# Linear attention layers and the input pass: normed rows and K turned in blocks of 32 by VectorE and moved by SBUF transfers, in place of TensorE transposes

## The reference

```
# block 0: 16 heads of 32; block 1: 8 heads of 64 (linear attention)
xn = layernorm(x)
q = softmax(xn @ Wq + bq, over a head's features)
k = softmax(xn @ Wk + bk with masked rows at -inf (block 1: -1e6), over the 512 rows)
v = (xn @ Wv + bv) * keep
attn = k^T v for each head;  y = q @ attn
x = x + silu(layernorm(y) * (1 + scale) + shift) @ Wo + bo
# block 2: the same frame with ordinary softmax attention, 16 heads
# block 3: xn = layernorm(layernorm(x) * ada_scale + ada_shift); products of xn (mx, delta,
# B, C rows); two selective state-space scans over the rows; gated output projection
```

## Time and profile before

| | |
|---|---|
| median of 3 runs | 5685.93 us (5684.82 to 5686.73) |
| the profiled execution | 5681.6 us |
| its span in the profile | 5679.5 us |
| mean granted TensorE clock | 0.989 of full |
| TensorE matmul busy | 5410.8 us (95%) |
| VectorE busy | 4209.2 us (74%) |
| ScalarE busy | 2919.1 us (51%) |
| GpSimd busy | 2906.6 us (51%) |

### The profile page before, as it was taken

How to read it: one execution, slowest core, us unless ns; L and a number is a source line. 1 busy time by engine, 2 the same in 40 slices (tenths; PEclk the granted TensorE clock), 3 DMA queues, 4 the chain that set the end, 5 groups by cost and what they waited for, 6 DMA issues and landing times. The chain is left out here.

```text
span 5679.5 us, 136465 instructions
## 1 busy us (share of the span) xinstructions
PE 5410.8 (95%) x58478; PEld 3262.1 (57%) x58478; DVE 4209.2 (74%) x5904; ACT 2919.1 (51%) x4944; POOL 2906.6 (51%) x956
## 2 busy tenths in 40 slices
PE   8999989998999999978989999999999999999998
PEld 3555545554455555544445566666666666666665
DVE  1456545554466666673349999999999999999996
ACT  0122212222455555551247776777777677677774
POOL 0000000000000000003449999999999999999997
PEclk9999999999999999998999999999999999999999
DMA  6200021001000000004431111112111121201211
GB/s 237 80 34 33 32 71 34 31 29 65 11 1 20 17 21 17 21 20 164 167 120 50 52 34 62 65 60 69 54 43 55 60 67 54 73 24 62 65 59 33
DMA packets 146330, 321.90 MB, mean 57 GB/s; under 512 B 27721, under 2 KB 28362, under 8 KB 135514
## 3 DMA queue, kind: packets, MB, share of 16 engines
q1 hardware_dynamic: 142866, 308.25, 16.1%
q10 hardware_dynamic: 2896, 5.34, 0.3%
HBM read 238.66 MB, written 74.89 MB: 55 GB/s over the span
## 5 line engine op out<-in xcount | busy, mean ns | idle before, releaser
L2070 POOL TENSOR_TENSOR sc_state<-sc_state,sc_c_rows 128x2048 f32<-128x2048 f32 x512 | 2330.2, 4564 | 122.8 <-DVE sc_state L2381 121.4
L2381 DVE TENSOR_TENSOR_SCAN sc_state<-sc_decay,wide 128x512 f32<-128x512 f32 x2048 | 2335.2, 1198 | 28.0 <-PE wide L2240 20.8
L2240 PEld LDWEIGHTS wide<-sc_diag,sc_du_t 64*64 64x64 f32 x32768 | 1048.0, 133 | 527.0 <-issue 344.0
L2240 PE MATMUL wide<-sc_diag,sc_du_t 64*64 64x128 f32 x32768 | 1218.9, 272 | 19.9 <-DVE sc_state L2381 19.7
L2256 PE MATMUL wide<-sc_state,half 64*64 64x512 f32 x8192 | 1199.5, 592 | 7.5 <-POOL sc_state L2070 7.0
L2174 ACT ACTIVATE sc_decay<-sc_delta,neg_a 128x512 f32<-128x512 f32 x1024 | 723.6, 719 | 448.7 <-DVE sc_state L2381 443.6
L2174 ACT ACTIVATE sc_decay<-sc_delta_x,neg_a 128x512 f32<-128x512 f32 x1024 | 710.1, 717 | 286.7 <-DVE sc_state L2381 282.5
L2256 PEld LDWEIGHTS wide<-sc_state,half 64*64 64x64 f32 x8192 | 405.8, 133 | 168.6 <-issue 127.5
L1491 DVE CUSTOM_DVE_ANT_0 l_prob<-wide,l_mask_add 128x512 f32<-128x512 f32 x512 | 339.6, 682 | 211.6 <-PE wide L1323 211.4
L1232 ACT ACTIVATE l_prob<-l_prob,l_s_max 128x512 f32<-128x512 f32 x512 | 366.0, 716 | 250.4 <-DVE l_s_max L1491 250.4
L2213 PE MATMUL wide<-set 128*128 128x512 f32 x1024 | 476.2, 608 | 0.0
(11 more groups left out here) (244 smaller groups left out, 6912.6 us busy)
## 6 DMA issues: line engine op xcount, KB each, us to landing
sc_c_rows<-c_d SPq DMA_DIRECT2D x64, 1024.0 KB, 4.8
set<-wz_tiles SPq DMA_DIRECT2D x128, 256.0 KB, 2.7
x<-ahead_out SPq DMA_DIRECT2D x24, 1024.0 KB, 4.8
ahead_x_wk<-x SPq DMA_DIRECT2D x16, 1024.0 KB, 5.7
sc_mx<-mx_d SPq DMA_DIRECT2D x64, 256.0 KB, 2.7
mx_d<-fr_mx SPq DMA_DIRECT2D x14, 1024.0 KB, 4.4
pro_wc<-in_wcT SPq DMA_DIRECT2D x4, 2048.0 KB, 19.2
xn_d<-fr_xn_t SPq DMA_DIRECT2D x8, 1024.0 KB, 4.2
```

Source lines behind the costliest of these rows:

```text
L2070: pool.tensor_tensor(state[quad % STATES][:, :, :], state[quad % STATES][:, :, :], c_rows[(r * 4 + q) % ROWS][:, :, :], ALU.mult).then_inc ...
L2240: last = pe.matmul(to[cols_to, k, :, :], du_t[slot % 2][rows, k, of * 64:(of + 1) * 64], diag[r % 2][rows, c, k, :, :], start=True, stop=True)
L2381: dve.tensor_tensor_scan(state[quad % STATES][:, step % 4, order], decay[step % DECAYS][:, order], pair[:, i, order], 0.0, ALU.mult, ALU.a ...
```

## The change

In the two linear layers the stages TK and T leave TensorE. VectorE instead turns blocks of 32x32 within a tile (`turn_x`, `turn_k`; four instructions of 128x512 each), and SyncE moves the blocks to their partitions with 16 SBUF-to-SBUF transfers of 64 KB for x (`move_x`) and 16 for K (`move_k`). Each transfer goes from 32 partitions to 32 partitions with runs of 128 floats (512 bytes). ScalarE then scales the moved rows from SBUF into `xn_t`, undoing the order of the blocks by its access pattern. K's features are dealt out by fours on the host (`by_fours`), so that K's turned blocks come out in runs of 128 floats as well. K is scaled by the reciprocal of its sums in both layers, by four VectorE instructions at the end of the batch before, and the drain of A loses the scale in layer 1. The first `xn` of a layer is still turned by TensorE, in the banks of stage Y. The input pass does the same for the normed rows of batches 1 to 7: VectorE turns them behind the normed rows, SyncE moves them (`move_blocks`), and ScalarE scales them (`scaled`) behind the seventh of the eight SiLU drains of the batch before.

```diff
-        plan = [("V", 4, "dve"), ("TK", 4, "act"), ("TQ", 4, "act"), ("A", 4, "dve"), ("Y", 4, "dve"),
-                ("T", 4, "act"), ("K", 4, "dve"), ("TY", 4, "act"), ("Q", 4, "dve"), ("O", 4, "dve")]
+        plan = [("V", 4, "dve"), ("TQ", 4, "act"), ("A", 4, "dve"), ("Y", 4, "dve"),
+                ("K", 4, "dve"), ("TY", 4, "act"), ("Q", 4, "dve"), ("O", 4, "dve")]
...
+                def move_x(b):
+                    sp.wait_ge(x_turned, (b + 1) * TT)
+                    for i in range(4):
+                        for q in range(4):
+                            sp.dma_start(xn[q * 32:(q + 1) * 32, :, i * P:(i + 1) * P],
+                                         x_blocks[i * 32:(i + 1) * 32, q, :, :, :].rearrange("c k t r -> c k (t r)")
+                                         ).then_inc(x_moved, 16)
+                def move_k(b):
+                    sp.wait_ge(k_turned, (b + 2) * DT)
+                    if not isinstance(b, int) or b >= 0:
+                        sp.wait_ge(psum_full, st.full(b, "A", DT - 1))
...
                         load(b + 2, j)
+                        move_x(b)
+                        move_k(b)
                     sp.wait_ge(out_ready, (b + 1) * TT)
...
                 def next_norms(b):
+                    act.wait_ge(x_moved, (b + 1) * 256)
+                    act.sem_inc(passed, 1)
+                    act.wait_ge(psum_full, st.full(b, "V", TT - 1))
                     for k in range(DT):
-                        drain(b, "T", k, xn_t[:, k, :], ACT.Identity, scale=col(NW, k), bias=col(NB, k))
+                        act.activation(xn_t[:, k, :].rearrange("p (t i r) -> p t i r", t=TT, i=4),
+                                       xn[:, k, :].rearrange("p (i t r) -> p t i r", t=TT, i=4), ACT.Identity,
+                                       scale=col(NW, k), bias=col(NB, k)).then_inc(xn_t_ready, 1)
...
                 def next_k(b):
-                    pe.wait_ge(xn_ready, (b + 2) * TT)
-                    transposes(pe, b, "T", xn)
-                    pe.wait_ge(*wait_drained(b, "T", DT - 1))
                     if isinstance(b, int) and b < 0:
+                        pe.wait_ge(xn_ready, TT)
+                        transposes(pe, b, "Y", xn)
                         pe.wait_ge(w_ready[1], 16)
+                    pe.wait_ge(xn_t_ready, (b + 2) * DT)
                     project_t(pe, b, "K", wk)
...
                     if linear:
-                        pe.wait_ge(k_norm_ready if layer == 0 else k_exp_ready, (b + 1) * DT)
-                        transposes(pe, b, "TK", k_t)
                         pe.wait_ge(q_exp_ready, (b + 1) * TT)
                         transposes(pe, b, "TQ", q_tm)
                         pe.wait_ge(v_ready, (b + 1) * TT)
-                        pe.wait_ge(*wait_drained(b, "TK", TT - 1))
+                        pe.wait_ge(k_moved, (b + 1) * 256)
...
+                def turn_x(b):
+                    for t in range(TT):
+                        dve.wait_ge(xn_ready, b * TT + t + 1)
+                        dve.sem_inc(passed, 1)
+                        dve.transpose(x_blocks[:, :, :, t, :].rearrange("p q k r -> p k q r"), xn[:, t, :]
+                                      ).then_inc(x_turned, 1)
+                def turn_k(b):
+                    dve.wait_ge(k_exp_ready, (b + 2) * DT)
+                    dve.sem_inc(passed, 1)
+                    dve.reciprocal(k_sum[:, :], k_sum[:, :]).then_inc(rk_ready, 1)
+                    dve.wait_ge(rk_ready, b + 2)
+                    for k in range(DT):
+                        dve.tensor_scalar(k_t[:, k, :], k_t[:, k, :], k_sum[:, k:k + 1], None, ALU.mult
+                                          ).then_inc(k_norm_ready, 1)
+                    if not isinstance(b, int) or b >= 0:
+                        dve.wait_ge(k_moved, (b + 1) * 256)
+                    for k in range(DT):
+                        dve.wait_ge(k_norm_ready, (b + 1) * DT + k + 1)
+                        dve.sem_inc(passed, 1)
+                        dve.transpose(k_blocks[:, :, :, :, k].rearrange("p q t r -> p t q r"), k_t[:, k, :]
+                                      ).then_inc(k_turned, 1)
...
                     norms(b + 1, pair + j, 1 - j)
...
+                    if not last:
+                        turn_x(b + 1)
...
                         next_k(b)
                         next_q(b)
+                        turn_k(b)
                     dve.wait_ge(xb_ready, b + 1)
...
+                    if b + 1 < B:
+                        move_blocks(b + 1)
                     parts = 4 if b == B - 1 else 2
...
+                def scaled(b):
+                    act.wait_ge(blocks_moved, b * 256)
...
+                        if m == 6 and b + 1 < B:
+                            scaled(b + 1)
...
+                    for t in range(TT):
+                        dve.wait_ge(xn_ready, b * TT + t + 1)
+                        dve.transpose(turned[:, :, :, t, :].rearrange("p j k r -> p k j r"), xn[j][:, t, :]
+                                      ).then_inc(blocks_turned, 1)
```

More of the change, by code:

```diff
@@ L490, in attention_layer @@
         pt_full, pt_ready, pv_done, y_drained = sem("pt_full"), sem("pt_ready"), sem("pv_done"), sem("y_drained")
+        x_turned, x_moved, k_turned, k_moved = sem("x_turned"), sem("x_moved"), sem("k_turned"), sem("k_moved")
+        xn_t_ready = sem("xn_t_ready")
         def wait_bank(pe, b, name, k):
@@ L680, in _ @@
                     sp.dma_start(scan["half"][:, :], d["half_ident"]).then_inc(scan["const_loaded"], 16)
+                def move_x(b):
[9 more added lines that the diff above has]
+                        sp.wait_ge(psum_full, st.full(b, "A", DT - 1))
+                    for i in range(4):
+                        for q in range(4):
+                            sp.dma_start(k_tm[q * 32:(q + 1) * 32, :, i * P:(i + 1) * P],
+                                         k_blocks[i * 32:(i + 1) * 32, q, :, :, :].rearrange("c t r m -> c t (r m)")
+                                         ).then_inc(k_moved, 16)
                 def body(b, pair, j, more):
@@ L783, in body @@
                     if linear:
-                        for t in range(TT):
-                            drain(b, "TK", t, k_tm[:, t, :], ACT.Copy)
                         for k in range(DT):
@@ L877, in body @@
                     project(pe, b, "O", h_t, wo)
-                first = [i[0] for i in plan].index("T")
+                first = [i[0] for i in plan].index("Y")
                 absent(st, pe, psum_full, "pe", -1, plan[0][0], first)
@@ L895, in _ @@
                 dve.sem_inc(xn_ready, TT)
-                first = [i[0] for i in plan].index("T")
+                first = [i[0] for i in plan].index("K")
                 absent(st, dve, drained["dve"], "dve", -1, plan[0][0], first)
@@ L921, in norms @@
                     dve.wait_ge(rstd_ready, b + 1)
-                    if not isinstance(b, int) or b > 0:
-                        dve.wait_ge(psum_full, st.full(b - 2, "T", DT - 1))
+                    dve.wait_ge(xn_t_ready, b * DT)
                     for t in range(TT):
@@ L958, in body @@
                     norms(b + 1, pair + j, 1 - j)
-                    if linear:
-                        dve.wait_ge(k_exp_ready, (b + 1) * DT)
-                        dve.reciprocal(k_sum[:, :], k_sum[:, :]).then_inc(rk_ready, 1)
-                        dve.wait_ge(rk_ready, b + 1)
-                        if layer == 0:
-                            for k in range(DT):
-                                dve.tensor_scalar(k_t[:, k, :], k_t[:, k, :], k_sum[:, k:k + 1], None, ALU.mult
-                                                  ).then_inc(k_norm_ready, 1)
+                    if not last:
+                        turn_x(b + 1)
                     for t in range(TT):
@@ L1030, in _ @@
                 next_q(-1)
+                turn_k(-1)
                 absent(st, dve, drained["dve"], "dve", -1, "O", 1)
@@ L2476, with by_fours @@
     s = lambda key: v["L3_cond_" + key]
+    def by_fours(layer, a):
+        return a if layer == 2 else a.reshape(a.shape[:-1] + (P, 4)).swapaxes(-1, -2).reshape(a.shape)
     def crossed(a):
```

89 lines of the change are left out of this document (55 added, 34 removed).

## The result

The changed kernel took 5713.16 us (median of 5 runs, 5709.2 to 5715.7), the kernel before 5685.93 us on the same chip: the ratio is 1.0045, with a 95% interval of 1.0031 to 1.0059. It is slower, where I had forecast 5614 us and at most 5660. The profiled execution after took a span of 5707.1 us, 27.6 more than the 5679.5 before.

What follows compares the result with a forecast made beforehand. TensorE, busy 96 to 97% in the changed stages, was taken as the bound. Gains of 48.7 + 17.7 + 5.0 + 0.9 = 72.3 us gave 5614 us; forecast 5590 to 5632, wider range 5588 to 5660.

Steps and rivals of the forecast that it cites:

- T's 3.48 us: Linear layers, end of Y to K: stage T with its drain goes, 3.48 us in each of 14 batches, 48.7 us.
- GpSimd's lock on V's scaling: Linear layers: the V scaling that meets GpSimd's addition takes 4.03 us instead of 0.49, standing still until GpSimd is done.
- The input pass's chain: Input pass: VectorE turns, SyncE moves, ScalarE scales the normed rows; it takes back TensorE's 25 us, leaving 0.9 us gained.
- its floor of 5590: Whole kernel: the time with every wait in the input pass gone, 24 us under the forecast of 5614.
- I take 0.45 per transfer: SyncE's queue: each small transfer issued 0.45 us after the last; the layers' wait stays hidden up to 0.56 us.
- GpSimd's addition waits for the store, but not before the next normed rows: Linear layers: the store queued behind K's 16 transfers on SyncE does not delay GpSimd's addition; costed at nothing.
- the first product should wait for ScalarE about 3 us per batch: Input pass, sign in the new trace: TensorE's first product waits about 3 us and the period stays near 38.3.
- A late by 1.9 or 3.7 us: First batch of each layer: turning K ahead of the norms makes A later by 1.9 in layer 0, 3.7 in layer 1.
- K by 4.3 in the rival: Linear layers, slower-queue rival: at an issue interval of 0.85 us K waits 4.3 us in each of 14 batches, 60 us.
- turning K: VectorE, first batch of a layer: four block transposes at 0.69 us each, within 4.85 us of added work before A.
- the forecast 71 us: Both linear layers: the summed gain, 48.7 from stage T, 17.7 from layer 0's V to A and 5.0 from layer 1's.
- The queue sets the pace: Rival on SyncE's transfers: issues every 0.85 us give 5716 us; queue slower than 0.6 had chance 0.28, of which 0.12 slower.

Runs made afterwards that it cites:

- e2: The changed kernel with the layers' store of each batch's result issued by ScalarE instead of SyncE behind K's 16 transfers: 5693.2 us, ratio 1.0012 to the kernel before.
- e8: The changed kernel with e3, e5 and e4 together, and half of the layers' transfers of x issued by ScalarE: 5604.5 us, ratio 0.986 to the kernel before.
- e5: e2 with VectorE's loop over the batches of the linear layers written out: 5672.6 us, ratio 0.9976 to the kernel before.
- e1: The changed kernel with its input pass put back as before the change, layers still changed: 5679.3 us, ratio 0.9988 to the kernel before.
- e4: The changed kernel with each 64 KB transfer written as one run of 2 KB per partition instead of four of 512 bytes: 5701.4 us, ratio 1.0027.
- e7: The changed kernel with half of the input pass's 16 transfers issued by ScalarE, half by SyncE: 5667.6 us, ratio 0.997 to the kernel before.
- e3: The changed kernel with the input pass's normalising and turning ahead of three drains, and its transfers ahead of three small stores: 5661.7 us, ratio 0.9959.
- e9: The changed kernel with only VectorE's loop of the linear layers written out, store left on SyncE: 5699.4 us, ratio 1.0023 to the kernel before.

## Why the prediction was wrong

**What held.** T's 3.48 us are gone and K follows Y, without a wait behind 11 of 14 batches. A block transpose of `x` takes 0.68 us, also under GpSimd's addition (e2). Landing is 2.0 to 2.1 us. GpSimd's lock on V's scaling is there. The input pass's chain is built as I wrote it. And the gain that I summed up is there to be had: e8, with its further edits, is 10 us under my forecast and 15 us above its floor of 5590.

**The step that failed first: "I take 0.45 per transfer".** It is 0.64 (10.3 us for 16). I read it from single issues at the start of a layer; no row showed sixteen in a row. By my own formula this alone costs 14 x (15 x 0.19 - 1.7) + 7 x 15 x 0.19 = 36 us: 5650, still faster than before and inside my range. What made it slower are three things that I costed at nothing or did not see.

**"GpSimd's addition waits for the store, but not before the next normed rows".** That sentence was true only with 7 us of issues in front of the store. With 10.3 us the addition comes 2.3 us late, A with it (V + 18.8 against V + 16.56 in e2), and in e2, which moves only the store, the time falls by 20 us. I had named the wait and not worked out its slack.

**The loop's turn, not in the prediction at all.** At the jump back VectorE stands 3.1 to 3.6 us instead of 0.67. It delays two batches of each layer and is worth 21 us once the store is on time (e2 to e5), 14 us with it late.

**"... the first product should wait for ScalarE about 3 us per batch", and nothing for the clock behind it.** In the layers too (A late by 1.9 or 3.7 us, K by 4.3 in the rival), I priced a wait at its length. All profiled executions of this study together, by the time that TensorE stood idle just ahead of the stage, and how often the stage then ran at 2.4 GHz's pace (A in 3.7 or 3.8 us; the input pass's first product in 3.6 or 3.7):

| idle ahead | A | first product |
|---|---|---|
| up to 1.0 us | 86 of 86 | 40 of 42 |
| 1.0 to 2.0 | 13 of 16 | 9 of 9 |
| 2.0 to 3.3 | 15 of 52 | 1 of 3 |
| over 3.3, to 9.3 | 0 of 54 | 0 of 50 |

The two slow first products with 0.9 us ahead stand in the kernel before and in e1, so idle time goes with most of the slow stages and not with all. The slow ones take 5.1 to 6.8 us, as 3.7 us of work does when part of it or nearly all runs at 1.2 GHz. In the changed kernel this is 21 us in A, 2 in the K behind layer 0's first batch, and 17 in the input pass. The window of the input pass above shows the same as a granted clock of 0.93.

**The layers' account.** My sum had A waiting 18 us for VectorE in both layers; it waits 52.6. A small part is a term that I mis-sized: turning K takes 3.86 us for four, not 2.76, and A waits 6.9 and 6.7 us in the two first batches instead of 5.4. With 34.5 us more waiting, 21 of slow A, and 8 at K (waits of 3.4, 2.2 and 0.8 us, and the slow one), 64 of the forecast 71 us are gone. That leaves 7; the trace shows 4 to 6, and e1 7. In the input pass 43.9 us of waiting and 17 of half clock stand against 7 x 3.6 that T gave back: +36, measured +35. So of the 99 us between forecast and result, about 40 are the slow clock, 40 are longer waits in the layers, and 20 are longer waits in the pass.

**The rival.** "The queue sets the pace" was right in kind and in sign, but by its own formula 0.64 us is under its balance of 0.76; it needed the clock, the store and the loop's turn to become true. I gave slower 0.12.

**Open.** What sets 0.64 us for an issue (not the runs; beside a large store it gets longer); why e4's median is 12 us lower and not 5; and whether it is the body's length that makes the jump dear.

## What to carry to other kernels

Work taken from the engine that sets the end pays only if the chain that takes its place arrives in time, and a wait there costs more than its length: here 3 to 6 us of idle TensorE were followed by 1.5 to 3 us of slow products. Count a burst of small DMAs by a burst that you have measured, and look at what stands behind it in the same queue (here one store, 20 us) before you call the queue idle. The cures were cheap: start the chain where its engine sits idle anyway (51 us), issue from a second engine (45 us), write out a loop at whose jump the engine stands (21 us).

## What the runs showed of the hardware

- An issue of a 64 KB transfer between two SBUF tiles takes its engine 0.60 us and comes every 0.64, with runs of 512 bytes or of 2 KB (0.63); two engines issue at the same time at a median of 0.65 each (e7). Beside other transfers 16 of them took up to 13.0 us (e3), and 11.8 where ScalarE issued a 1 MB store meanwhile (e2).
- At the jump back of its loop VectorE stands 0.62 to 0.67 us in one kernel and 3.1 to 3.6 us in the other, whose body is longer; written out, 0.15 (e5, e9).
- A block transpose of 128x512 takes 0.68 us and is not held by GpSimd's addition, where a scaling of the same size is. The one that writes `k_blocks` in steps of four elements takes 1.09.
